# Links from step rows, scaled segments ahead of the copies, and two gather tiles by indirect DMA

## The chip, the cores and the metric

The kernel runs on one core of one Trainium2 chip. The metric is the time of one execution on the device in microseconds; the time before is the median of three runs. In the profile, PE is TensorE's matmul, PEld its weight load, DVE is VectorE, ACT is ScalarE, POOL is GpSimd and SP is SyncE, which here only issues DMAs.

## The reference

There are 256 nodes with 512 features and 4352 edges (`src`, `dst`, sorted by `dst`). Four layers follow each other, each on the layer norm of `x` and added to `x`:

```python
# layer 1: diffusion over the graph
h = x @ W + b
adj = zeros(256, 256); adj[src, dst] = 1; adj[dst, src] = 1; adj += eye
adj = adj / max(adj.sum(1), 1)
out = dw[0] * h; cur = h
for i in range(3):
    cur = adj @ cur; out += dw[i + 1] * cur
x = x + relu(out)
# layer 2: 16 experts of width 64, weighted by a two-level routing
x = x + sum_e tw[:, e] * ((silu(xn @ W1[e]) * (xn @ W3[e])) @ W2[e])
# layer 3: 64 paths over the edges; a segment is 32 of the 512 features
x1 = xn[src]                                  # gather, 4352 rows
for p in range(64):
    edge_out[:, i3[p]] += coef[p] * x1[:, i1[p]] * x2[:, i2[p]]
x = x + zeros(256, 512).at[dst].add(edge_out) # scatter
# layer 4: a mixture with 64 small experts, each picks one of 16 tokens
```

What matters for the change is `adj` in layer 1 (a 1 wherever any edge has that source and destination, however many edges do) and the gather and the products of layer 3.

## The kernel before

All five engines have a program of their own, written out by hand in order, and synchronise by semaphores. An instruction waits at the head of its engine's queue, and what stands behind it waits too.

**Layer 1.** The edges form 34 tiles of 128. For each tile VectorE makes two one-hot matrices in bf16, 128 edges by 256 nodes: `src_oh` (L644) and `dst_ohb` (L646), by comparing the row 0..255 (`iota_b`) with the edge's index. TensorE's `count` (L1008) adds up `src_oh`^T `dst_ohb` over all tiles in two banks, so that each entry counts the edges of a pair. `link_b` (L666) is this count compared with 0.5. TensorE adds its transpose (L1044, L1045), VectorE makes `adj` and its row sums (L683), `cmat` (the rows scaled, L691), and the two series matrices; `square` (L1032) makes the higher powers, and the diffusion is one product `series` x `cur` (L1055), where `cur` is the projection `h` (L1023) plus the bias (L694, L708). `project` is eight pairs of matmul instructions, four for each half of the nodes. TensorE's queue holds, in this order: broadcasts of the source indices (L999), sixteen fillers `keep_warm` (L976, a matmul with zeros), counts of tiles 0 to 8, the transposes of `xn` (L984), counts of tiles 9 to 16, six projections, counts of tiles 17 to 33, symmetric sum, two projections, two squares, diffusion. `src_t` (L674) is the transposed source one-hot for the gather, made from the broadcasts for ten tiles.

Then VectorE and ScalarE form the next layer norm (L716, L626, L451, L634) while TensorE runs 34 fillers, transposes the first half, runs 6 more, and transposes the second half.

**Layer 2.** Eight chunks of 128 hidden features: TensorE makes gate and up (L1073), ScalarE the Silu (L489), VectorE the product (`hidden`, L813) and the routing weight (L828, four in all); the down projection is 32 instructions L1097, sixteen for each half of the nodes, each chunk a pair. Behind the last Silu ScalarE loads the square-root table again (L492) and takes the root for each half of the nodes (L451).

**Gather.** `xn` is written to DRAM (`xn_rows`, L366) and split into three bf16 parts (`xparts`). The tiles of block 0, ten, are gathered by TensorE: six matmuls L1102 for each tile (two halves of the nodes times three parts). Eight tiles have a bank each: first all tiles' first half, then the second half part by part, and tiles 8 and 9 at the end. ScalarE copies the even tiles (L502), VectorE the odd ones (L850) to `x1g[0]`. Ahead of the copies ScalarE converts five destination one-hots to fp32 (L507, `dst_oh`) and VectorE clears `rest_sums[1]` (L845). The tiles of blocks 1 and 2 come from `xn_rows` by GpSimd's indirect DMA (L424, `gather_rows`), one for each tile.

**Path blocks.** Blocks of 10, 14 and 10 tiles. For each of the 64 paths a product goes to one of 12 slots. A path is either direct, where VectorE multiplies both segments and the coefficient in one operation (L874), or ScalarE scales the edge segment into the slot (L526) and VectorE multiplies it with the gathered segment (L879). The first `DIRECT[b]` paths of a block are direct, 16, 16 and 0 before. TensorE adds the product of the first `KEPT[b]` tiles (8, 6, 4) to the bank sums (L1178, L1181), VectorE adds the rest (L889) in SBUF. The scatter matmuls of the block before (L1129) are spread over the paths of the next. Between two blocks ScalarE copies the bank sums out (`copy_sums`, L536, L541). Slots lie in `prod` (5), `xn` (2), `xparts` (3) and `src_t` (2).

**Layer 4** and the store follow; the change leaves them as they are.

## Time and profile before

| | us |
|---|---|
| median of 3 runs | 295.93 (295.72 to 295.97) |
| the profiled execution, its own time | 295.56 |
| its span, first to last instruction | 293.3 |
| diffusion ends / gate and up matmuls start | 36.06 / 43.9 |
| first product of block 0 / of block 1 | 101.08 / 139.66 |
| VectorE busy / ScalarE busy / TensorE busy | 223.4 / 141.3 / 278.1 |

An engine's share is no measure of what it holds up: a stage has to be read where it ends. Fillers count as busy TensorE. The durations below come from the profiled execution; where an engine overlaps two instructions, a row shows the full time of each, and the pitch is read from the starts of neighbours.

### The profile page before, as it was taken

What the parts mean: (1) busy time and instruction counts of PE and PEld (TensorE: products, weight loads), DVE (VectorE), ACT (ScalarE), POOL (GpSimd) and SP (SyncE); (2) the same over time, 40 slices, a digit from 0 to 9 for tenths busy, and PEclk for the clock granted to TensorE, in tenths of its full rate; (3) what the DMA queues carried; (4) which work ended last, traced back from release to release, by engine and by line L of the source; (5) the groups of instructions that cost most, each with busy time, mean ns of one, the idle gap of its engine ahead of it and who ended that gap; (6) DMA issues with size and microseconds to landing.
All of it is one profiled execution on the core that took longest, in us unless ns stands there. A gap on an engine that the chain in (4) does not pass through costs nothing.

```text
span 293.3 us, 5671 instructions
## 1 busy us (share of the span) xinstructions
PE 278.1 (95%) x1711; PEld 193.5 (66%) x1711; DVE 223.4 (76%) x644; ACT 141.3 (48%) x279; POOL 36.7 (13%) x49
## 2 busy tenths in 40 slices
PE   4897799999999899999999999999999999999995
PEld 3754498888444388999678777665666654578632
DVE  5977648243256899999999999999999987955221
ACT  3200132110224358992538786579989819422220
POOL 3000030023003770000870000000000000000000
PEclk9999999999999999999999999999999999999999
DMA  6699960000002774242452000004544429000001
GB/s 206 233 407 420 428 296 0 0 2 1 0 36 70 198 201 140 79 141 76 131 158 72 2 1 1 2 16 136 154 145 144 146 77 349 6 0 2 2 2 72
DMA packets 12287, 33.39 MB, mean 114 GB/s; under 512 B 3297, under 2 KB 3298, under 8 KB 12002
## 3 DMA queue, kind: packets, MB, share of 16 engines
q1 hardware_dynamic: 10338, 26.73, 25.2%
q0 software_dynamic: 1920, 6.29, 7.5%
q8 instruction: 15, 0.25, 0.3%
q14 instruction: 14, 0.11, 0.1%
HBM read 31.97 MB, written 1.05 MB: 113 GB/s over the span
## 4 chain that ended last, share of the span: by engine, by line
PE 82%; DVE 7%; ACT 5%; issue 2%; DVEq 1%; DMA 1%; ACTq 0%; SPq 0%
PE psum L1178 15%; PE psum L1129 12%; PE psum L1073 10%; PE psum L1181 7%; PE psum L1097 5%; PE psum L1102 4%; PE psum L976 4%; PE psum L1008 3%; PE psum L1244 3%; PE psum L1257 2%; PE psum L1263 2%; PE psum L1023 2%; PE psum L1136 2%; DVE big L889 2%; PE psum L1169 1%
## 5 line engine op out<-in xcount | busy, mean ns | idle before, releaser
L1129 PE MATMUL psum<-big,dst_oh 128*128 128x512 f32 x104 | 48.8, 593 | 0.0
L526 ACT ACTIVATE prod<-edges,coef_b 128x320 f32 (+1 forms) x65 | 35.7, 588 | 12.8 <-PE psum L1181 10.7
L879 DVE TENSOR_TENSOR prod<-big,prod 128x320 f32<-128x320 f32 (+1 forms) x65 | 34.8, 535 | 0.5 <-issue 0.3
L424 POOL DMA_INDIRECT big<-xn_rows,big x24 | 26.9, 1119 | 59.3 <-DVE prod L879 29.0
L1178 PE MATMUL psum<-prod,ident 128*128 128x128 f32 x160 | 31.8, 296 | 0.2 <-DVE prod L879 0.2
L1178 PEld LDWEIGHTS psum<-prod,ident 128*128 128x128 f32 x160 | 23.9, 190 | 7.9 <-issue 6.6
L1073 PE MATMUL psum<-edges,big 128*128 128x256 f32 x128 | 28.3, 380 | 0.0
L1129 PEld LDWEIGHTS psum<-big,dst_oh 128*128 128x128 f32 x104 | 18.0, 191 | 13.5 <-issue 13.4
L889 DVE TENSOR_TENSOR big<-big,prod 128x64 f32 (+2 forms) x80 | 26.6, 333 | 0.0
L1073 PEld LDWEIGHTS psum<-edges,big 128*128 128x128 f32 x128 | 24.1, 190 | 3.5 <-DVE edges L813 0.3
L526 ACT ACTIVATE xparts<-edges,coef_b 128x320 f32 (+1 forms) x41 | 22.6, 587 | 2.9 <-PE psum L1181 1.6
L879 DVE TENSOR_TENSOR xparts<-big,xparts 128x320 f32<-128x320 f32 (+1 forms) x41 | 21.9, 534 | 0.5 <-issue 0.3
L1178 PE MATMUL psum<-xparts,ident 128*128 128x128 f32 x96 | 19.5, 298 | 0.8 <-DVE xparts L879 0.7
L1181 PE MATMUL psum<-prod,ident 128*128 128x128 f32 (+1 forms) x110 | 19.9, 262 | 0.0
L526 ACT ACTIVATE xn<-edges,coef_b 128x320 f32 (+1 forms) x26 | 14.8, 589 | 4.0 <-PE psum L1181 3.6
L1181 PEld LDWEIGHTS psum<-prod,ident 128*128 128x128 f32 x110 | 16.7, 192 | 0.0
L1178 PEld LDWEIGHTS psum<-xparts,ident 128*128 128x128 f32 x96 | 14.1, 190 | 3.7 <-issue 3.2
L889 DVE TENSOR_TENSOR big<-big,xparts 128x192 f32 (+2 forms) x48 | 16.3, 339 | 0.0
L976 PE MATMUL psum<-iota_b,zero_b 128*128 128x256 bf16 x118 | 16.2, 293 | 0.0
L526 ACT ACTIVATE src_t<-edges,coef_b 128x320 f32 (+1 forms) x28 | 15.6, 584 | 1.0 <-PE psum L1178 0.6
L879 DVE TENSOR_TENSOR src_t<-big,src_t 128x320 f32<-128x320 f32 (+1 forms) x28 | 14.9, 532 | 0.0
L489 ACT ACTIVATE edges<-psum 128x256 f32<-128x256 f32 x8 | 3.1, 384 | 24.2 <-PE psum L1073 18.6
(199 smaller groups left out, 510.8 us busy)
## 6 DMA issues: line engine op xcount, KB each, us to landing
big<-in_w SPq DMA_DIRECT2D x3, 2048.0 KB, 16.1
edges<-in_f SPq DMA_DIRECT2D x11, 512.0 KB, 3.3
edges<-in_edge SPq DMA_DIRECT2D x1, 3584.0 KB, 23.9
edges<-in_edge SPq DMA_DIRECT2D x1, 2560.0 KB, 23.4
edges<-in_edge SPq DMA_DIRECT2D x5, 512.0 KB, 3.5
edges<-in_f SPq DMA_DIRECT2D x1, 2560.0 KB, 9.9
big<-in_gnn_w SPq DMA_DIRECT2D x1, 1024.0 KB, 6.3
xs<-in_x SPq DMA_DIRECT2D x1, 512.0 KB, 3.9
```

What stands on the lines that cost most here:

```text
L424: nc.gpsimd.indirect_dma_start(out=x1g[b % 2][:, i, :], out_offset=None, in_=xn_rows, in_offset=bass.IndirectOffsetOnAxis(ap=idx_i[:, 0, F ...
L526: nc.scalar.activation(slot(n)[:, 0:BLOCKS[b], :], segment(edges[:, FIRST[b]:FIRST[b] + BLOCKS[b], :], single_column(words, p)), ACT.Copy, ...
L879: nc.vector.tensor_tensor(v, segment(xg[:, 0:tiles, :], first_column(words[b], p)), v, ALU.mult).then_inc(mults, 1)
L889: nc.vector.tensor_tensor(v, v, slot(n)[:, KEPT[b]:BLOCKS[b], :], ALU.add).then_inc(sums, 1)
L976: mm(to[:, 0:N], zero_b[:], iota_b[:], start=True, stop=True)
L1008: last = mm(bank[4 + h][:, 0:N], src_oh[:, t, h * P:(h + 1) * P], dst_ohb[:, t, :], start=t == 0, stop=t == T - 1)
L1073: last = mm(bank[2 + c % 4][:, n * N:(n + 1) * N], w[:, kc, c * P:(c + 1) * P], xnT[:, kc, :], start=kc == 0, stop=kc == KC - 1)
L1097: last = mm(bank[2 + h], hT[:, c, h * P:(h + 1) * P], w2_sb[:, c, :], start=c == 0, stop=c == HC - 1)
L1102: last = mm(gather_bank(t), src_t[:, h, t * P:(t + 1) * P], xparts[:, k, h, :], start=h == 0 and k == 0, stop=h == H - 1 and k == 2)
L1129: last = mm(bank[2 + h], dst_oh[:, n % DR, h * P:(h + 1) * P], tile_sums(b, t), start=False, stop=False)
L1178: last = mm(path_sums(to), ident[:], product[:, 0:PT].rearrange("p t u -> p (t u)"), start=False, stop=False, skip_group_check=True)
L1181: last = mm(more_sums(b, to), ident[:], product[:, PT:KEPT[b]].rearrange("p t u -> p (t u)"), start=False, stop=False, skip_group_check=True)
```

## The change

1. **Steps in place of one-hots for the links.** The destination one-hot is replaced, for the counts, by a row of 258 columns that changes its value behind column `dst` (`steps`). ScalarE makes it by Sign for two tiles in three (+1 and -1), VectorE by a comparison for the third (1 and 0). A column of the sum differs from its right neighbour exactly where an edge ends in it, so `link_b` is now the comparison of the counts with their copy shifted by one (`shifted`, in the place of `cmat`). The destination one-hots, which the scatters need, are made later, behind `hidden(4)` to `hidden(7)`.
2. **TensorE's order in layer 1.** Six fillers at the start in place of sixteen between broadcasts; counts 9 to 17, one projection, counts 18 to 33, two projections, symmetric sum, two, square, two, square, one, diffusion. The fillers in front of the next transposes are 29 and 2 in place of 34 and 6. VectorE's order behind `cmat` follows.
3. **Gather.** TensorE gathers eight tiles; tiles 8 and 9 of block 0 come by two indirect DMAs at the head of GpSimd's queue. The second half's second and third part run tile by tile. Half of `rest_sums[1]` is cleared by GpSimd.
4. **Direct paths** are 0, 8 and 0. ScalarE scales paths 0 to 3 ahead of its gather copies; the first two slots are now free parts of `prod`, the next two lie in `xn`. The five `dst_oh` conversions and ScalarE's path words stand ahead of the third table load.

```diff
-    PE_TILES = BLOCKS[0]
+    PE_TILES = 8
-    DIRECT = [16, 16, 0]
+    DIRECT = [0, 8, 0]
+    FREE_SLOTS = 2
-    OH_A, OH_B = 5, 9
+    OH_A, OH_B = 7, 9
+    STEP_W = N + 2
...
+        def by_vector(t):
+            return t % 3 == 2
...
             def gather_rows(b):
-                if b == 1:
+                if b == 0:
                     pool.wait_ge(xn_out, 16 * H)
-                else:
+                if b == 2:
                     pool.wait_ge(mults, NP * (b - 1))
-                for i in range(BLOCKS[b]):
+                for i in range(0 if b else PE_TILES, BLOCKS[b]):
...
             nc.gpsimd.memset(rest_sums[0], 0.0).then_inc(cleared[0], 1)
+            nc.gpsimd.memset(rest_sums[1][:, 4:, :], 0.0).then_inc(cleared[1], 1)
...
+            gather_rows(0)
             gather_rows(1)
             gather_rows(2)
```

ScalarE:

```diff
             nc.scalar.activation(root[:, H:H + 1], eps[:], ACT.Sqrt)
-            copy_broadcast(0, QT)
+            scalar_tiles = [t for t in range(T) if not by_vector(t)]
+            def make_steps(lo, hi):
+                for t in scalar_tiles[lo:hi]:
+                    nc.scalar.activation(steps[:, t, :], iota_w[:], ACT.Sign, bias=idx_f[:, 2, t:t + 1], scale=-1.0)\
+                        .then_inc(steps_a, 1)
+            act.wait_ge(idx_ready, 3)
+            make_steps(0, 8)
             for h in range(H):
                 root_of_variance(0, h)
+            copy_broadcast(0, 2)
+            make_steps(8, 12)
             copy_xnT(0, xnT)
...
+            make_steps(12, T)
+            copy_broadcast(2, QT)
+            act.wait_ge(cnt_ps, 1)
+            nc.scalar.activation(shifted[:, 0, :], bank[4][:, 1:N + 1], ACT.Copy).then_inc(shift_a, 1)
...
+            act.wait_ge(packed, 3)
+            words = load_words(act, ROW_PATHS, COL_PATHS)
+            act.wait_ge(dst_hot, T)
+            for n in range(DR):
+                nc.scalar.activation(dst_oh[:, n, :], dst_ohb[:, scatter_tile[n], :], ACT.Copy).then_inc(dst_made, 1)
             nc.scalar.activation(root[:, H:H + 1], eps[:], ACT.Sqrt)
...
-            act.wait_ge(onehot, 2 * T)
-            for n in range(DR):
-                one_hot(n)
-            for t in range(0, BLOCKS[0], 2):
+            for n in range(FREE_SLOTS + XN_SLOTS):
+                scale(n)
+            for t in range(0, PE_TILES, 2):
                 copy_gathered(t)
```

VectorE:

```diff
             def one_hots(lo, hi):
                 for t in range(lo, hi):
                     nc.vector.tensor_scalar(src_oh[:, t, :], iota_b, idx_f[:, 0, t:t + 1], None, ALU.is_equal)\
                         .then_inc(onehot, 1)
-                    nc.vector.tensor_scalar(dst_ohb[:, t, :], iota_b[:], idx_f[:, 1, t:t + 1], None, ALU.is_equal)\
-                        .then_inc(onehot, 1)
+                    if by_vector(t):
+                        nc.vector.tensor_scalar(steps[:, t, :], iota_w[:], idx_f[:, 2, t:t + 1], None, ALU.is_le)\
+                            .then_inc(steps_v, 1)
...
-            for h in range(H):
-                dve.wait_ge(cnt_ps, 1)
-                nc.vector.tensor_scalar(link_b[:, h, :], bank[4 + h][:, 0:N], 0.5, None, ALU.is_gt).then_inc(link_ready, 1)
+            dve.wait_ge(cnt_ps, 1)
+            nc.vector.tensor_copy(shifted[:, 1, :], bank[5][:, 1:N + 1]).then_inc(shift_v, 1)
+            for h in range(H):
+                dve.wait_ge((shift_a, shift_v)[h], 1)
+                nc.vector.tensor_tensor(link_b[:, h, :], bank[4 + h][:, 0:N], shifted[:, h, :], ALU.is_gt)\
+                    .then_inc(link_ready, 1)
...
+                if c >= 4:
+                    dst_one_hots((c - 4) * T // (HC - 4), (c - 3) * T // (HC - 4))
...
-            nc.vector.memset(rest_sums[1], 0.0).then_inc(cleared[1], 1)
+            nc.vector.memset(rest_sums[1][:, 0:4, :], 0.0).then_inc(cleared[1], 1)
...
                     if b == 0:
-                        dve.wait_ge(gathered, copied_before(tiles))
-                        dve.wait_ge(xn_out, 16 * H)
+                        dve.wait_ge(gathered, PE_TILES // 2)
+                        dve.wait_ge(row_in[b], 16 * (tiles - PE_TILES))
```

TensorE:

```diff
-                        keep_warm(bank[5], ((34, 6), (18, 2))[stage - 1][h])
+                        keep_warm(bank[5], ((29, 2), (18, 2))[stage - 1][h])
...
+            pe.wait_ge(const, 2)
+            keep_warm(bank[3], 6)
...
-                if q == 2:
-                    keep_warm(bank[3], 16)
...
-            count(OH_B, T // 2)
-            project(0, 0, KC)
-            project(1, 0, KC // 2)
-            count(T // 2, T)
+            count(OH_B, 18)
+            pe.wait_ge(xnT_ready, 2)
+            pe.wait_ge(w_in, 16)
+            project(0, 0, 1)
+            count(18, T)
+            project(0, 1, 3)
             pe.wait_ge(link_ready, H)
...
-            project(1, KC // 2, KC)
+            project(0, 3, KC)
+            project(1, 0, 1)
             square(bank[1], adj, cmat, s2_ps, cmat_ready)
+            project(1, 1, KC - 1)
             square(bank[4], cmat, series2, s3_ps, series2_ready)
-            pe.wait_ge(h_ready, H)
+            project(1, KC - 1, KC)
...
-            for k in range(3):
-                pe.wait_ge((part_a, part_a, part_r)[k], (3, 4, 4)[k])
-                for t in range(8):
-                    gather_part(t, 1, k)
-            for t in range(8, BLOCKS[0]):
-                gather(t)
+            pe.wait_ge(part_a, 3)
+            for t in range(8):
+                gather_part(t, 1, 0)
+            pe.wait_ge(part_a, 4)
+            pe.wait_ge(part_r, 4)
+            for t in range(8):
+                gather_part(t, 1, 1)
+                gather_part(t, 1, 2)
```

## Rows read from the trace of the kernel before

**Rows 1.** The page's part 4, shares of the span by engine.
```profile
PE 82%; DVE 7%; ACT 5%; issue 2%; DVEq 1%; DMA 1%; ACTq 0%; SPq 0%
```

**Rows 2.** Windows by stage: stretch, length, each engine's busy us (instructions), clock, DMA.
```profile
core 0: us, PE busy (x) PEld busy (x) DVE busy (x) ACT busy (x) POOL busy (x), PEclk, DMA share, GB/s
101.00:111.90 10.90, 10.79 (x68) 8.28 (x66) 10.55 (x31) 5.27 (x10) 7.40 (x8) 1.00 0.71 196
111.90:139.60 27.70, 27.25 (x195) 25.16 (x194) 26.93 (x97) 20.93 (x39) 0.06 (x1) 1.00 0.33 104
139.60:154.60 15.00, 15.00 (x92) 10.34 (x91) 14.78 (x32) 7.27 (x14) 12.25 (x10) 1.00 0.51 146
154.60:194.00 39.40, 38.59 (x257) 29.87 (x256) 39.40 (x92) 29.57 (x56) 0.04 (x1) 1.00 0.04 13
```

**Rows 3.** The chain that ended last, piece by piece: start us, us, what.
```profile
4.76 3.41 PE psum L976 x16
...
14.24 5.15 PE psum L1023 x12
...
19.39 3.73 PE psum L1008 x34
...
26.42 1.90 PE psum L1032 x8
...
32.39 3.67 PE psum L1055 x8
...
36.06 3.71 PE psum L976 x34
...
86.99 12.96 PE psum L1102 x60
...
195.33 0.91 ACT xparts L526 x2
```

**Rows 4.** Timeline, first 40 us: start us, us, engine, line, operation.
```profile
0.73 1.28 ACT L467 ACT_TABLE_LOAD   x1 [0.73 <-PEq L1285]
...
3.25 0.26 DVE L650 CAST idx_f<-big 128x68 f32<-128x68 int32 x1 [3.25 <-DMA big<-in_dst]
...
19.73 0.29 DVE L644 TENSOR_SCALAR big<-iota_b,idx_f 128x256 bf16<-128x256 bf16 x1
...
19.93 0.29 DVE L646 TENSOR_SCALAR big<-iota_b,idx_f 128x256 bf16<-128x256 bf16 x1
...
23.21 0.76 DVE L666 TENSOR_SCALAR edges<-psum 128x256 bf16<-128x256 f32 x2 [2.99 <-PE psum L1008]
...
38.54 0.55 DVE L634 TENSOR_SCALAR xn<-xs,mv,rstd 128x512 f32<-128x512 f32 x1
```

**Rows 5.** Groups by form, 101 to 140.5 us: line, operation, count, busy us, mean ns.
```profile
L526 ACT ACTIVATE prod<-edges,coef_b 128x320 f32 x20 | 11.1, 562 | 7.6 <-PE psum L1181 6.6 <-issue 0.3
...
L879 DVE TENSOR_TENSOR prod<-big,prod 128x320 f32<-128x320 f32 x20 | 9.8, 490 | 0.3 <-issue 0.3
...
L874 DVE SCALAR_TENSOR_TENSOR prod<-big,coef_b,edges 128x320 f32 x9 | 4.9, 550 | 0.6 <-DVE big L850 0.4
```

**Rows 6.** Timeline from the down projection to the gather.
```profile
73.10 13.90 PE L1097 MATMUL psum<-big,edges 128*128 128x512 f32 x32
...
73.71 0.42 DVE L813 TENSOR_TENSOR edges<-edges,psum 128x256 f32<-128x256 f32 x1 [3.03 <-ACT edges L489]
...
74.24 0.69 DVE L828 TENSOR_TENSOR edges<-edges,psum 128x512 f32<-128x512 f32 x1
...
81.83 0.29 ACT L451 ACTIVATE root<-mv,eps 128x1 f32<-128x1 f32 x1 [6.64 <-DVE mv L627]
...
91.73 1.62 ACT L507 ACTIVATE dst_oh<-big 128x256 f32<-128x256 bf16 x5
```

**Rows 7.** Timeline of the gather and the first products.
```profile
93.82 0.95 POOL L424 DMA_INDIRECT big<-xn_rows,big  x1 [0.30 <-issue]
...
101.08 1.01 DVE L874 SCALAR_TENSOR_TENSOR prod<-big,coef_b,edges 128x320 f32 x2 [0.41 <-DVE big L850]
```

**Rows 8.** DMA issues by line, with the median us from issue to landing.
```profile
big<-xn_rows,big POOLq DMA_INDIRECT x24, 3.8
```

More of the change, by code:

```diff
@@ L107, in extra_slots @@
             return room[:, 0:n * BMAX * U].rearrange("p (s t u) -> p s t u", s=n, u=U)
-        slots = [prod[:, i] for i in range(OWN_SLOTS)]
-        for room, n in ((xn[:].rearrange("p h d -> p (h d)"), XN_SLOTS),
-                        (xparts[:].rearrange("p k h d -> p (k h d)").bitcast(F32), PART_SLOTS),
+        slots = [prod[:, i] for i in range(OWN_SLOTS - FREE_SLOTS, OWN_SLOTS)]
+        slots += [extra_slots(xn[:].rearrange("p h d -> p (h d)"), XN_SLOTS)[:, i] for i in range(XN_SLOTS)]
+        slots += [prod[:, i] for i in range(OWN_SLOTS - FREE_SLOTS)]
+        for room, n in ((xparts[:].rearrange("p k h d -> p (k h d)").bitcast(F32), PART_SLOTS),
                         (src_t[:].rearrange("p h n -> p (h n)").bitcast(F32), SLOTS - OWN_SLOTS - XN_SLOTS - PART_SLOTS)):
@@ L152, in graph_and_experts @@
         sum_room = [take([BLOCKS[0], D]), late_sums]
-        dst_ohb = take([T, N], BF16)
+        step_room = take([T * STEP_W], BF16)
+        steps = step_room.rearrange("p (t n) -> p t n", n=STEP_W)
+        dst_ohb = step_room[:, 0:T * N].rearrange("p (t n) -> p t n", n=N)
         idx_i = take([2, T], I32)
@@ L713, in _ @@
                     .then_inc(series_ready, 1)
+            dve.wait_ge(h_ps, 2)
+            nc.vector.tensor_tensor(cur[:, 1, :], bank[3], bias_b, ALU.add).then_inc(h_ready, 1)
             for h in range(H):
@@ L1005, in count @@
                 for t in range(lo, hi):
-                    pe.wait_ge(onehot, 2 * (t + 1))
+                    pe.wait_ge(onehot, t + 1)
+                    if by_vector(t):
+                        pe.wait_ge(steps_v, sum(by_vector(i) for i in range(t + 1)))
+                    else:
+                        pe.wait_ge(steps_a, sum(not by_vector(i) for i in range(t + 1)))
                     for h in range(H):
-                        last = mm(bank[4 + h][:, 0:N], src_oh[:, t, h * P:(h + 1) * P], dst_ohb[:, t, :],
+                        last = mm(bank[4 + h][:, 0:STEP_W], src_oh[:, t, h * P:(h + 1) * P], steps[:, t, :],
                                   start=t == 0, stop=t == T - 1)
@@ L1011, in count @@
                     last.then_inc(cnt_ps, 1)
-            for q in range(QT):
-                if q == 2:
-                    keep_warm(bank[3], 16)
+            for q in range(2):
                 broadcast(q)
@@ L1018, in _ @@
             transpose_xn(0)
-            pe.wait_ge(w_in, 16)
+            for q in range(2, QT):
+                broadcast(q)
             def project(h, lo, hi):
@@ L1105, in gather_part @@
                     last.then_inc(gat_ps, 1)
-            def gather(t):
-                if t % 2 == 0:
-                    pe.wait_ge(gathered, copied_before(t - 7))
-                else:
-                    pe.wait_ge(gathered_odd, (t - 7) // 2)
-                for h in range(H):
-                    for k in range(3):
-                        gather_part(t, h, k)
             def scatter(b, n, t):
@@ L1170, in _ @@
                     for _ in range(2 if b else 0):
-                        mm(bank[4][:, 0:N], zero_b[:], iota_b[:], start=False, stop=False, skip_group_check=True)
+                        mm(bank[4][:, 0:N], zero_b[:], iota_b, start=False, stop=False, skip_group_check=True)
                 for p in range(NP):
@@ L1184, in _ @@
                     if KEPT[b] > PT and b and p % 2:
[L1185 removed]
+                        mm(bank[4][:, 0:N], zero_b[:], iota_b, start=False, stop=False, skip_group_check=True)
                     if p in scatter_at:
```

87 lines of the change are left out of this document (46 added, 41 removed).

## The prediction

> **What bounds the kernel now.** I read the chain that ended last first: TensorE holds four fifths of it [rows 1]. A share is an average, so I then read the chain piece by piece over the first 45 us, where most of the edit lies [rows 3], the timeline around its operations [rows 4, 6, 7], and the stages of the path blocks with the busy time of each engine [rows 2]. The reader is to see four places. (a) Up to 23.12 us the counts L1008 wait in TensorE's queue behind twelve projection instructions L1023 (5.15 us), although VectorE had made its last one-hot at 20.2 us [rows 3, 4]. (b) From 23.12 us to the end of the diffusion matmuls at 36.06 us TensorE waits twice for VectorE: 0.9 us for the links and 1.5 us before L1055. (c) Sixty gather matmuls follow the down projection, 12.96 us [rows 3], and the first product starts only at 101.08 us [rows 7]. (d) In block 0 and block 1 VectorE is busy nearly all the time: 10.55 of 10.90, 26.93 of 27.70, 14.78 of 15.00, 39.40 of 39.40 us [rows 2]. TensorE looks as busy there, but its groups only follow the products. The gate and up matmuls, the down projection, block 2 and the last stage are TensorE's own work and the edit leaves them.
>
> **Part 1, links by steps.** VectorE made 68 one-hots before the counts could end, one each 0.20 us [rows 4]. Now it makes 34 source one-hots and 11 step rows, 45 in all, and one small cast more: 23 x 0.197 = 4.5 us less, so it ends at 20.2 - 4.5 + 0.2 = 15.9 us. ScalarE gets 23 Sign activations of 128x258 with a bias column. No row shows Sign. Nearest from below: the 128x256 copies L507, five in 1.62 us, 0.32 us each [rows 6]; from above: the 128x320 scaling L526 with a scale column, 0.56 us alone [rows 5] and 0.455 us each in a pair that runs without waits [rows 3]. Its form is the nearer one; 62 columns fewer leave 0.41 us, which I take: 23 x 0.41 = 9.4 us. ScalarE starts them at 3.9 us (indices at 3.25 us and three small VectorE operations), and between them lie two roots (0.5), two broadcast copies (1.1) and two copies of xnT (1.1), with a wait for the transposes of about 0.3: 3.9 + 9.4 + 3.0 = 16.3 us. The counts are now fed from both engines, and with one projection pair ahead of them instead of twelve instructions they end at about 16.7 us, against 23.12. With 0.32 us a row VectorE decides and it is 16.3; with 0.50 it is 18.4.
>
> Behind the counts I add up TensorE's new order in the durations of [rows 3]: projections 1.72, symmetric sum 0.6, projections 1.72, square 1.90, projections 1.72, square 1.90, last projection 0.86, together 10.4 us, then L1055 3.67 us: 14.1 us to the end of the diffusion against 36.06 - 23.12 = 12.9 before. VectorE must stay under this cover. The link now takes a copy (0.42) and two compares behind it, 1.2 us instead of 0.8 [rows 4]; the projections hide it, and would cost 0.4 us if they didn't. The first half of h is added before the second square ends; the second half is late by about what the first L1055 pair takes. So the diffusion ends at 16.7 + 14.1 = 30.8 us: 5.3 us earlier.
>
> The fillers L976 between diffusion and transposes go from 34 and 6 to 29 and 2. Before, the first transposes followed the fillers at 39.8 us [rows 3], while their input was finished at 39.1 us [rows 4]. Five fillers fewer (0.55 us) are given back nearly whole, and of four fewer in the second group (0.44 us) a part is waited for the second half's input, which follows the first by 0.65 us: together 0.65 us. Part 1 gives 5.9 us, between 4.0 (Sign at 0.50) and 6.3.
>
> **What is moved under the expert stage.** The 34 destination one-hots (34 x 0.197 = 6.7 us) now stand behind hidden(4) to hidden(7), some 1.7 us each. VectorE has room: it idles 3.03 us before the last L813. What is queued behind the last nine is the weighting L828, at 74.24 us now, then at about 76.0, done 76.7. The down projection starts at 73.10 us and needs it for its thirteenth instruction, at 73.10 + 12 x 0.43 = 78.3 us [rows 6]: 1.6 us of cover. ScalarE gets the path words, the wait for the one-hots and five copies (1.62 us) ahead of its table load (1.28): free at about 79.3, needed at 81.83 [rows 4, 6]. I cost all of it at nothing; without the cover it would be at most 1.8 us. GpSimd's longer memset lies in its idle time.
>
> **Part 2, two tiles by GpSimd.** Twelve gather matmuls of 0.216 us go: 2.6 us [rows 3]. The second half's parts are now finished tile by tile, so the copies spread over the matmuls: the last copy follows the last matmul as before (0.69 us), then 0.41 us to the first product. The first product, counted from the same start of the gather, moves from 101.08 to 98.4 us, 2.7 us. It now needs the two rows too. The queue's second indirect DMA was issued at 93.82 us; at 3.8 us to landing the second lands at 97.6 [rows 7, 8], 0.8 us before it is wanted, so nothing; a landing 1 us later would cost 0.2 us. Every DMA of block 1 stands 2.5 us later in GpSimd's queue; that queue is empty from 111.9 to 139.6 us [rows 2], which hides it. SyncE's queue keeps its order; its transfers for block 2 wait for counts of products and so move with them. VectorE's memset ahead of the copies is halved, so it cannot cost.
>
> **Part 3, no direct paths in block 0, eight in block 1.** ScalarE scales four paths before its gather copies (it waited there), the rest behind them. Block 0's first 16 paths took 10.9 us, 0.68 each; the other 48 took 27.7, 0.577 each [rows 2]. 16 x 0.10 = 1.6 us. From below, the bare difference of the operations, 550 against 490 ns [rows 5], would give 1.0 us. ScalarE must scale one path per 0.577 us; a pair takes 0.91 us [rows 3], so it stays ahead, with slots to spare. Block 1: 16 direct paths in 15.0 us, 0.94 each; the next 46 in 39.4, 0.86: 8 x 0.08 = 0.6, of which I take 0.5, as ScalarE copies bank sums at that block's start.
>
> **The page that speaks against.** Rows: the square-root table was loaded once, 1.28 us, and Copy ran behind it without another load [rows 4]. The Trainium skill, "ScalarE: Activation LUTs", section "Table sets: the hidden batching unit", says that cheap functions (it names relu, copy, identity and abs) are in every set and that each set switch costs a load; it doesn't name sign there. By that rule, if Sign had a set of its own, the time would be as in rival 1; no run here shows it yet.
>
> **Sum.** 5.9 + 2.7 + 1.6 + 0.5 = 10.7 us off the profiled span of 293.3: 282.6. That execution took 295.56 us, 2.3 more than its span, so 284.9; the median, 295.93, lies 0.4 higher: 285.2 us.
>
> **Rivals.**
> 1. Sign needs another table than Sqrt. ScalarE's order is Sign, Sqrt, Sign; the first load hides before the indices, two of 1.28 us lie in its sequence, which sets the counts' end: +2.6, 287.8 us. For it: no Sign in the trace. Against it: Copy and Relu needed no load.
> 2. The clock rises late. TensorE ran the first 16 fillers at 0.213 us and later ones at 0.109 [rows 3], which is its 1.2 and its 2.4 GHz level (the granted clock column shows 1.00 throughout). Sixteen fillers at 4.76 us become six at 2.1 us, and TensorE then idles about 1 us for the normalisation. If the counts behind that run at the lower level, the 32 last ones cost 0.1 us more each: +3.4, 288.6 us.
> 3. The other side: the same level holds up to the diffusion's end. Counts, projections, squares and diffusion behind the transposes are about 20 us at the upper level [rows 3]; doubled, less 2 us of waits: +18, 303 us. It turns slower once more than 10.7 of these 20 us run at the lower level. Against it: once the counts come slower than their inputs, TensorE is busy without a gap, which is what raised the clock before.
> 4. The gather's gain is lost: rows or VectorE's word load arrive 2.7 us late, 287.9 us. Point of decision: the second row 3.5 us later than now, or ScalarE unable to keep 0.577 us a path.
>
> **How the numbers follow.** The forecast 285.2 has 0.70 (own range 283.2 to 287.0: part 1 between 4.0 and 6.3, part 3 between 1.0 and 2.5). Rival 1 0.10, rival 2 0.08, rival 4 0.08, rival 3 0.03, an unnamed loss of the whole gain 0.01. A range of 283.0 to 288.5 leaves out less than 2 in 10. This kernel can be told from no change from about 0.2% (0.6 us) on. Only rival 3 lies on the slower side: faster 0.96, no change 0.01, slower 0.03.
>
> **What would show it.** Right: L1008 ends near 16.7 us with the last Sign just before; diffusion ends near 31; L1097 starts near 67; the first product comes 11.4 us behind its end, not 14.1; DVE pitch in block 0 0.577 us from the first path. Wrong: a table load between Signs, L1008 at 0.21 us each behind the transposes, the first product released by a DMA, VectorE in block 0 waiting for ScalarE, or L1097 waiting for L828.

## The result, and the profile after

| | before | after |
|---|---|---|
| median, us | 295.83 (295.63 to 295.97, 4 runs) | 282.95 (282.94 to 282.96, 4 runs) |
| after / before | | 0.9565, 95% interval 0.9549 to 0.9582 |
| profiled execution: own time, span | 295.56, 293.3 | 282.94, 281.1 |
| counts end | 23.12 | 16.38 |
| diffusion ends | 36.06 | 30.19 |
| gate and up matmuls start | 44.05 | 37.32 |
| gather starts | 86.99 | 80.27 |
| first product | 101.08 | 91.58 |
| block 1's first product | 139.66 | 127.99 |
| block 2's first product | 196.54 | 184.35 |

The change is 12.9 us faster. I forecast 10.7 us and 285.2 us; the time lies 0.05 us below my range (283.0 to 288.5) and 2.25 us below the forecast.

The moments are read from the chain of work that ended last; the timeline puts the first gate and up matmul 0.15 us earlier, at 43.89 and 37.17 us, and the experiments below are compared by it.

The lines that answer to those of before follow. First the shares of the chain that ended last [rows 1]: the bound is where it was.

```profile
PE 84%; DVE 7%; ACT 5%; issue 2%; DVEq 1%; DMA 1%; ACTq 0%; SPq 0%
```

The same chain, piece by piece, up to the gather and the first product [rows 3] (start us, us, what):

```profile
9.79 2.17 PE psum L1064 x18
11.96 0.87 PE psum L1078 x2
12.84 3.54 PE psum L1064 x32
16.38 1.72 PE psum L1078 x4
...
26.50 0.86 PE psum L1115 x2
...
27.37 2.81 PE psum L1115 x6
30.19 3.17 PE psum L1026 x29
...
80.27 10.38 PE psum L1162 x48
90.64 0.02 issue
90.67 0.70 DVE big L900
91.37 0.14 issue
```

L1064 are the counts, L1078 the projections, L1115 the diffusion, L1026 the fillers, L1162 the gather. Two things are to be seen. The pieces from 9.79 us to the end of the diffusion follow each other without a hole, where before TensorE waited three times for VectorE: 0.92 us for the links, 0.58 us before the second square and 1.51 us before the diffusion. (The prediction names only the first and the third.) And each pair of the last counts takes 3.54 / 16 = 0.22 us, the same pace as when the counts were never late [rows 3]: TensorE waits for nobody there.

The timeline of that stretch [rows 4] shows the new engine at work (start us, us, engine, line, operation):

```profile
0.74 1.28 ACT L483 ACT_TABLE_LOAD   x1 [0.74 <-PEq L1337]
...
3.74 3.31 ACT L489 ACTIVATE big<-iota_w,idx_f 128x258 bf16<-128x258 bf16 x8 [1.26 <-DVE idx_f L697]
...
6.96 0.58 ACT L467 ACTIVATE root<-mv,eps 128x1 f32<-128x1 f32 x2
...
8.40 1.70 ACT L489 ACTIVATE big<-iota_w,idx_f 128x258 bf16<-128x258 bf16 x4
8.48 1.31 PE L1034 MATMUL psum<-ident,xn 128*128 128x128 f32 x8 [0.18 <-DVE xn L672]
...
10.95 4.51 ACT L489 ACTIVATE big<-iota_w,idx_f 128x258 bf16<-128x258 bf16 x11
...
15.28 0.27 DVE L682 TENSOR_SCALAR big<-iota_w,idx_f 128x256 bf16<-128x256 bf16 x1
...
16.41 0.42 DVE L710 COPY edges<-psum 128x256 f32<-128x256 f32 x1 [0.86 <-PE psum L1064]
```

A Sign takes 4.51 / 11 = 0.41 us, and Sign, Sqrt and Sign follow each other with no table load between them. The load at 0.74 us is ScalarE's only one before 35.01 us. The last Sign ends at 15.46 us and VectorE's last one-hot at 15.55 us, both ahead of the counts' end at 16.38.

Under the expert stage the destination one-hots stand ahead of the weighting (L878, which was L828) [rows 6]:

```profile
57.99 4.24 DVE L691 TENSOR_SCALAR big<-iota_w,idx_f 128x256 bf16<-128x256 bf16 x8
...
66.37 10.04 PE L1157 MATMUL psum<-big,edges 128*128 128x512 f32 x23
...
68.27 1.84 DVE L691 TENSOR_SCALAR big<-iota_w,idx_f 128x256 bf16<-128x256 bf16 x9
70.03 0.67 DVE L878 TENSOR_TENSOR edges<-edges,psum 128x512 f32<-128x512 f32 x1
70.15 1.64 ACT L527 ACTIVATE dst_oh<-big 128x256 f32<-128x256 bf16 x5 [3.19 <-DVE big L691]
```

The path blocks [rows 2]: stretch, length, busy time of each engine, clock, DMA share.

```profile
91.58:100.70 9.12, 9.12 (x70) 8.07 (x70) 9.12 (x33) 9.12 (x21) 6.99 (x8) 1.00 0.69 198
100.70:128.00 27.30, 26.96 (x193) 24.93 (x193) 26.48 (x97) 20.77 (x39) 4.83 (x6) 1.00 0.51 157
```

VectorE (the third column of busy times) works the whole of the first stretch, and ScalarE beside it. The first stretch holds the products of seventeen paths, not sixteen, so a pitch (the time from one path's product to the next one's) has to be read from the start of the seventeenth product. Here it is after the change, and then before it:

```profile
100.27 0.49 DVE L929 TENSOR_TENSOR prod<-big,prod 128x320 f32<-128x320 f32 x1
```
```profile
111.92 0.48 DVE L879 TENSOR_TENSOR prod<-big,prod 128x320 f32<-128x320 f32 x1
```

With the milestones of the table: the first sixteen paths take 8.69 us, 0.543 each, where they took 10.84, 0.678 each. The next forty-eight, which the edit doesn't touch, take 27.72 us and took 27.74, 0.578 each. So all of block 0's gain lies in its first sixteen paths.

### The profile page after: what moved, and what is told of

The parts are those of the page before. It is cut to its first block, busy times and chain, and to the rows that moved or that the text cites. A ratio compares the mean times of both kernels' runs of the same rounds, so it can differ in the third digit from the quotient of the medians.

```text
span 281.1 us, 5714 instructions
## 1 busy us (share of the span) xinstructions
PE 271.3 (96%) x1678; PEld 188.9 (67%) x1678; DVE 223.6 (80%) x654; ACT 160.7 (57%) x325; POOL 45.2 (16%) x52
## 4 chain that ended last, share of the span: by engine, by line
PE 84%; DVE 7%; ACT 5%; issue 2%; DVEq 1%; DMA 1%; ACTq 0%; SPq 0%
PE psum L1230 16%; PE psum L1179 13%; PE psum L1133 10%; PE psum L1233 8%; PE psum L1157 5%; PE psum L1162 4%; PE psum L1026 3%; PE psum L1296 3%; PE psum L1309 3%; PE psum L1315 3%; PE psum L1078 2%; PE psum L1186 2%; PE psum L1064 2%; DVE big L939 2%; PE psum L1221 2%
## 5 line engine op out<-in xcount | busy, mean ns | idle before, releaser
L564 ACT ACTIVATE prod<-edges,coef_b 128x320 f32 (+1 forms) x77 | 43.2, 594 | 10.3 <-PE psum L1233 8.8
L437 POOL DMA_INDIRECT big<-xn_rows,big x26 | 33.5, 1288 | 52.0 <-DMA xn_rows<-xn 23.5
L929 DVE TENSOR_TENSOR prod<-big,prod 128x320 f32<-128x320 f32 (+1 forms) x77 | 40.5, 527 | 0.7 <-ACT prod L564 0.3
L564 ACT ACTIVATE xparts<-edges,coef_b 128x320 f32 (+1 forms) x45 | 24.4, 586 | 1.5 <-PE psum L1230 0.9
L929 DVE TENSOR_TENSOR xparts<-big,xparts 128x320 f32<-128x320 f32 (+1 forms) x45 | 23.5, 522 | 0.3 <-issue 0.3
L1233 PE MATMUL psum<-prod,ident 128*128 128x64 f32 (+1 forms) x110 | 19.8, 262 | 0.0
L564 ACT ACTIVATE xn<-edges,coef_b 128x320 f32 (+1 forms) x32 | 17.8, 591 | 0.2 <-PE psum L1230 0.2
L929 DVE TENSOR_TENSOR xn<-big,xn 128x320 f32<-128x320 f32 (+1 forms) x32 | 16.8, 525 | 0.1
L564 ACT ACTIVATE src_t<-edges,coef_b 128x320 f32 (+1 forms) x30 | 16.4, 581 | 0.6 <-PE psum L1230 0.6
L1233 PEld LDWEIGHTS psum<-prod,ident 128*128 128x128 f32 x110 | 16.7, 192 | 0.0
L929 DVE TENSOR_TENSOR src_t<-big,src_t 128x320 f32<-128x320 f32 (+1 forms) x30 | 15.6, 521 | 0.2 <-ACT prod L564 0.2
```

The source lines that it names most:

```text
L437: nc.gpsimd.indirect_dma_start(out=x1g[b % 2][:, i, :], out_offset=None, in_=xn_rows, in_offset=bass.IndirectOffsetOnAxis(ap=idx_i[:, 0, F ...
L564: nc.scalar.activation(slot(n)[:, 0:BLOCKS[b], :], segment(edges[:, FIRST[b]:FIRST[b] + BLOCKS[b], :], single_column(words, p)), ACT.Copy, ...
L929: nc.vector.tensor_tensor(v, segment(xg[:, 0:tiles, :], first_column(words[b], p)), v, ALU.mult).then_inc(mults, 1)
L1233: last = mm(more_sums(b, to), ident[:], product[:, PT:KEPT[b]].rearrange("p t u -> p (t u)"), start=False, stop=False, skip_group_check=True)
```

## The experiments

There were sixteen runs, in four groups of four, each group on a chip of its own with the kernel before beside it. Before took 300.05, 300.07, 299.04 and 295.25 us in the four groups, not 295.83 in all: why, is the subject of the third group. So a time below stands beside the others of its group, and a part is read from the moments of its own trace (the table's rows above) where something else disturbs the time.

### Group 1: the parts of the first stage, and direct paths

**e1, all steps on VectorE.**
```diff
         def by_vector(t):
-            return t % 3 == 2
+            return True
```


> All 34 step rows on VectorE instead of 23 on ScalarE; everything else as in the changed kernel. Theory A (the gain of the first stage needs the work taken from VectorE): VectorE's 23 rows more, 0.197 us each, end its part at 15.6 + 4.5 = 20.1 us, the counts end at about 20.4 instead of 16.4, and the time is 282.95 + 4.0 = 287.0 us. Theory B (the gain is TensorE's new order alone, the counts being fed in time anyway): the counts end within 0.5 us of now, and the time stays under 283.5 us.

297.19 us (before 300.05). The counts end at about 20.6 us, and gate and up start at 41.40 and not 37.17 (timeline): ScalarE's 23 Signs are worth 4.2 us.

**e2, the old order on TensorE** (twelve projections ahead of the counts' second half, then both squares).
```diff
-            count(OH_B, 18)
+            count(OH_B, T // 2)
...
-            project(0, 0, 1)
-            count(18, T)
-            project(0, 1, 3)
+            project(0, 0, KC)
+            project(1, 0, KC // 2)
+            count(T // 2, T)
```


> TensorE's queue in the first stage as before the change (six projections ahead of the second half of the counts, the last two behind the symmetric sum), the step rows as in the changed kernel. Theory A (both halves of the edit are needed; in the changed kernel TensorE never waits behind the transposes, so only moved waits count): the counts end 4.3 us later (five projection pairs), the links' wait and the wait for the row-scaled matrix come back, and of the 5.9 us at the diffusion's end 3 to 4 are lost: 286 to 287 us. Theory B (the order is worth nothing, the freed VectorE is all): under 283.5 us.

296.37 us. TensorE's timeline shows the waits of before at their old places, and gate and up start at 40.31 us, 3.1 us late:

```profile
16.62 3.93 PE L1064 MATMUL psum<-big 128*128 128x258 bf16 x34
21.81 0.23 PE L1101 MATMUL psum<-edges 128*128 128x128 bf16 x1 [1.26 <-DVE edges L713]
...
26.98 1.99 PE L1087 MATMUL psum<-xparts,edges 128*128 128x256 f32 x8 [0.89 <-DVE xparts L751]
```

Taking away the steps loses 4.2 us and taking away the order 3.1; together the two gave 5.87 us at the end of the diffusion. So each without the other gives only 2.8 and 1.7 us: either edit alone leaves some of the other's wait.

**e3, the old numbers of fillers** (34 and 6 for 29 and 2).
```diff
-((29, 2), (18, 2))
+((34, 6), (18, 2))
```


> 34 and 6 fillers ahead of the second transposes again instead of 29 and 2. Theory A: in the changed kernel the transposes wait 0.2 us for the normalised half, so of nine fillers (0.97 us) 0.8 to 0.9 come back: 283.8 us. Rival (the fillers lie in a wait): 282.95 us.

294.16 us. Gate and up start at 38.03 against 37.17 us: the nine fillers are worth 0.86 us, not the 0.65 of my sum.

**e4, sixteen direct paths in block 0** (the ninth to the twenty-fourth).
```diff
-            return p < DIRECT[b]
+            return p < DIRECT[b] or (b == 0 and 8 <= p < 24)
```


> Paths 8 to 23 of block 0 are direct again (sixteen, as before the change, but eight paths later, so that ScalarE's start is as in the changed kernel). Theory A: VectorE sets the pitch of block 0, 0.68 against 0.567 us a path: + 1.8 us, 284.75 us. Rival (part of block 0's 2.2 us came from the paths prepared ahead of the copies, not from the form): + 1.0 us by the durations alone, 283.95 us.

293.17 us, and e3 less its 0.86 us of fillers comes to the same, 293.3, with all of block 0 scaled. The trace told why the part couldn't be read here: for some 10 us from about 98 us on (102 in e1 and e2) TensorE, VectorE and ScalarE stood nearly still in all four traces of the group. e15 repeats the edit without that.

### Group 2: the gather

**e5, the second half by parts and not tile by tile**: the loops over `t` and `k` in (1, 2) change places. 

> The second half of the gather runs part by part again (all eight tiles for the second part, then all for the third) instead of tile by tile; eight tiles as in the changed kernel. Theory A (the order spreads the copies over the matmuls): the copies start 1.7 us before the end of the matmuls instead of 3.2 and four of 0.6 us stand in each engine, so the first product comes 0.5 us later: 283.45 us. Rival (the copies keep up either way, or the rows of the indirect DMAs set the first product): 282.95 us.

293.36 us (before 300.07). The first product starts at 92.08 us against 91.58: three of VectorE's four copies stand in the chain, behind the forty-first of the 48 gather matmuls.

```profile
80.33 9.03 PE psum L1162 x41
89.36 0.02 issue
89.38 1.90 DVE big L900 x3
91.28 0.73 issue
```

The copies pile up, as the order by parts finishes the tiles together; tile by tile only one is left. The order is worth 0.5 us.

**e6, ten tiles by TensorE.**
```diff
-    PE_TILES = 8
+    PE_TILES = 10
```
with the matmuls of tiles 8 and 9 behind those of the eight. 

> TensorE gathers all ten tiles of block 0 again, tiles 8 and 9 behind the others; the indirect DMAs of block 0 are gone. Theory A: twelve matmuls of 0.216 us more and a copy behind them: the first product 2.6 us later, 285.55 us. Two broadcasts and their share of the transposed one-hot more in the first stage lie beside other work. Rival (the rows of the indirect DMAs arrive just when wanted, so that the gather was worth less): 284 us.

291.98 us, the fastest of its group, though the first product starts at 94.16 us, 2.6 us late. GpSimd issues 14 indirect DMAs in a row here and not 16, and the stretch in which the other engines stand cost 4 us less: 6.1 us against e16, which is this kernel without it, where it costs the changed kernel 10.0 (group 3).

**e7, six tiles by TensorE, four by GpSimd** (`PE_TILES = 6`, the loops over eight tiles cut to it). 

> TensorE gathers six tiles, GpSimd four by indirect DMA. Theory A (the rows are the next limit): the fourth indirect DMA is issued at 89.6 us, lands 3.8 us later at 93.4, and the first product waits for it until about 93.6 instead of 91.58: 285 us, slower than the changed kernel though TensorE has 2.6 us less to do. Rival (rows come in time or the product is not held): 280.4 to 282 us.

295.00 us. Here the rows are late, and the trace names it:

```profile
89.60 0.94 POOL L437 DMA_INDIRECT big<-xn_rows,big  x1 [0.30 <-issue]
```
```profile
93.59 0.89 DVE L929 TENSOR_TENSOR prod<-big,prod 128x320 f32<-128x320 f32 x2 [3.89 <-DMA big<-xn_rows,big]
```

The fourth row is issued at 89.60 us and the product starts 4.0 us later, 2.0 us after that of the change. With two tiles the second DMA is issued at 87.10 us; with the same 4.0 us it lands at 91.1, 0.5 us before the product. My sum had 0.8 us of cover. A third DMA, issued at 88.35 us, would land at about 92.3 by the same price, later than the change's first product; that is an estimate, as no run has three tiles.

**e8, nine one-hots made twice, ahead of the last weighting.**
```diff
+                if c == 7:
+                    for t in range(25, T):
+                        nc.vector.tensor_scalar(dst_ohb[:, t, :], iota_b, idx_f[:, 1, t:t + 1], None, ALU.is_equal)...
```


> The last nine destination one-hots, behind the last product of the expert stage, are made twice, which puts 1.9 us of VectorE's work ahead of the last routing weight. Theory A (cover of 1.0 us: in the changed kernel the weight is done at 70.70 us and the thirteenth instruction of the down projection needs it at 71.7): + 0.9 us, 283.85 us. Theory B (cover of 1.6 us, as predicted): + 0.3 us, 283.25 us. Theory C (the weight is not waited for at all): 282.95 us.

294.67 us. The added one-hots take 1.84 us, the down projection waits 0.96 us for the weighting, and the first product moves by 1.23 us, to 92.81: the moved one-hots hide with 0.6 to 0.9 us to spare, not the 1.6 of the prediction.

```profile
72.66 5.85 PE L1162 MATMUL psum<-big,edges 128*128 128x512 f32 x13 [0.96 <-DVE edges L883]
```

### Group 3: the stretch that disturbed the runs

**e9, the changed kernel unedited; e10, the kernel before unedited**, on one chip; e10 is a single execution, for its trace. 

> The changed kernel, unedited, on the chip of the other runs, on which the kernel before took 300.05 us and not 295.83. In all runs so far TensorE, ScalarE and VectorE crawl together from about 97 us to the end of GpSimd's row of indirect DMAs (109.4 us with 2+14 of them, 105.7 with 14): single instructions with 1 to 6 us between them and nothing that released them. If that belongs to this chip and not to my edits, the changed kernel shows it here too: 293.2 us (the run with more fillers, 294.16, less the 0.86 us that they measured), stages up to 97 us as in its first profile. If the edits caused it, 283 to 284 us and no crawl.

> The kernel before, unedited, for its trace on this chip. If the crawl comes from the row of indirect DMAs, it is seen here too, but shorter, as the row (14, from 92.1 us) ends at about 112 us and the first product starts only at 101.1: some 4 us lost between 103 and 112 us, 300 us in all, and everything up to 101 us as in [rows 3, 6, 7]. If it comes from something else, the 4 us are spread over the span.

**e11, block 1's indirect DMAs issued one for every four products.**
```diff
                 for i in range(0 if b else PE_TILES, BLOCKS[b]):
+                    if b == 1 and i:
+                        pool.wait_ge(mults, 4 * i)
                     nc.gpsimd.indirect_dma_start(
```


> One edit: block 1's indirect DMAs are issued one for every four products of block 0 and not back to back, the last at about 121 us, before block 1's first product at 128. Theory: the crawl comes from that dense row; then it is gone or nearly so and the time is 283.0 to 285 us on this chip. Rival: the crawl has another cause (a place in the code, the chip's clock); then it stays where it is, 293 us. Second rival: it lasts as long as any of the DMAs run, now until 121 us, and the time is over 300 us.

The changed kernel took 292.97 us here, 10 us more than in its first runs, and the kernel before 299.04 (299.10 in e10). Spread over block 0, the DMAs brought it to 282.92 us (0.9455 of before, interval 0.9439 to 0.9471). The windows of e9 and then of e11 show the stretch and its end:

```profile
92.00:97.50 5.50, 5.50 (x43) 4.64 (x43) 5.50 (x20) 3.43 (x8) 4.28 (x5) 1.00 0.70 192
97.50:109.30 11.80, 3.39 (x13) 2.52 (x13) 2.87 (x10) 1.42 (x3) 7.11 (x8) 0.64 0.68 198
109.30:115.00 5.70, 5.70 (x32) 5.70 (x31) 4.94 (x18) 5.70 (x14) 0.00 (x0) 0.56 0.24 61
```
```profile
97.50:109.30 11.80, 11.61 (x85) 10.69 (x84) 11.53 (x42) 11.29 (x23) 5.49 (x5) 1.00 0.59 167
```

In 11.8 us TensorE issued 13 matmuls in e9 and 85 in e11; VectorE and ScalarE fell with it, and only GpSimd went on, with eight DMAs at its usual pace and the DMA engines 68% busy. The waits of e9 in that stretch name no releaser inside the core (engine and line, what it waited for, us in total, times, longest):

```profile
ACT xn L564 <- remote: 5.8, 1, 5.8
DVE xn L929 <- ACT xn L564: 5.8, 1, 5.8
PEld psum L1233 <- issue: 4.7, 4, 1.8
...
PE psum L1233 <- issue: 4.4, 4, 1.7
```

"issue" is time in which an engine waits for nothing that the profile shows. The last DMA of e9's row is issued at 105.79 us, and the engines run again from 109.3:

```profile
105.79 0.95 POOL L437 DMA_INDIRECT big<-xn_rows,big  x1 [0.30 <-issue]
```

TensorE's clock falls with it: 0.64 of 2.4 GHz granted over the slow stretch, in which it was busy 3.4 of 11.8 us, and 0.56 in the 5.7 us behind it, close to the level of 1.2 GHz. The kernel before shows the same in e10, from about 106 to 112 us, shorter as its row is: up to its first product (100.82 us) it is as in [rows 7], and block 0 takes 42.4 us for 38.6. So the stretch is a matter of the dense row, in three of the groups; it isn't the edit's. The change only makes it cost more, as its row has two DMAs more and lies beside products for 17 us (92.0 to 109.3) and not 11.5 (100.8 to 112.3): 10 us of its time, and some 4 of before's.

What starves the engines isn't shown. The first runs of the changed kernel issued the same row at the same pace and lost nothing. A supply of instructions that the row holds up would fit waits without a releaser, but no run tests it; nor does one tell the chip from the hour or from where the data lay, since each group had its own.

**e12, the spread and two edits more**: no direct paths in block 1 (with the copies of block 0's banks ahead of its ninth path), and the normalisation behind two one-hots fewer.
```diff
-    DIRECT = [0, 8, 0]
+    DIRECT = [0, 0, 0]
-    OH_A, OH_B = 7, 9
+    OH_A, OH_B = 5, 7
```


> The spread of e11, and two edits more whose places don't touch: no direct paths in block 1, and the normalisation behind five and seven one-hots, not seven and nine. Block 1 against e11: eight direct paths of 0.94 us each become 0.86: 0.5 us earlier, if ScalarE keeps 0.86 us a path; if its bank copies get in the way, nothing. Counts: their end moves from 16.38 by 0.2 us at most by my reading that TensorE is busy without a gap behind the transposes and VectorE's last one-hot (15.55 us) holds it next; if the normalisation alone set it, by 0.6 us. Together 0.5 to 1.1 us less than e11.

285.90 us, 3 us slower than e11 where 0.5 to 1.1 us faster was expected. The earlier normalisation ends the counts 0.35 us later, at 16.73: the transposes start only 0.23 us earlier (8.25 for 8.48), and four count matmuls that ran ahead of them now run behind. In block 1 ScalarE stands still with block 2's row of DMAs running, and VectorE waits for it:

```profile
136.57 0.67 ACT L566 ACTIVATE prod<-edges,coef_b 128x448 f32 x1 [0.68 <-remote]
143.08 0.67 ACT L566 ACTIVATE prod<-edges,coef_b 128x448 f32 x1 [5.84 <-remote]
```
```profile
143.95 0.62 DVE L931 TENSOR_TENSOR prod<-big,prod 128x448 f32<-128x448 f32 x1 [3.63 <-ACT prod L566]
```

Either the row, or ScalarE's lack of room, could be behind it. The last group decides on the second.

### Group 4: the parts undisturbed

Before, with its dense row, took 295.25 us on this chip, so the stretch seems to be absent here anyway. In the four runs block 1's row is spread, and none of their traces shows it.

**e13, both rows spread** (block 2's DMAs too, one for every four products). 

> Block 1's and block 2's indirect DMAs both one for every four products. Against the spread of block 1 alone (282.92 us): in block 2's dense row one DMA on GpSimd took 6.39 us where the others took 0.94 to 1.56; if that too is the crawl, falling on GpSimd itself, it is gone, and as VectorE didn't wait for it the time stays within 0.4 us of 282.9. If block 1's direct paths and ScalarE's bank copies have nothing to do with the row, the same time as well; this run is the base for the next one.

**e14, the same without direct paths in block 1**, the copies of block 0's banks ahead of the ninth path.
```diff
-    DIRECT = [0, 8, 0]
+    DIRECT = [0, 0, 0]
...
-                if b == 1 and p == 0:
+                if b == 1 and p == 8:
                     copy_sums(0, 0, 8)
```


> Both rows spread, and no direct paths in block 1 (its first eight are scaled by ScalarE; the copies of block 0's banks stand before the ninth). In the run before, with block 2's row dense, ScalarE stood still for 5.84 us behind 137.2 us, VectorE waited 3.63 us for it, and the kernel lost 3 us. Theory: that standstill is the crawl again, falling on ScalarE; with the row spread it is gone and eight paths at 0.86 and not 0.94 us give 282.3 to 282.9. Rival: ScalarE has no room there for eight more scalings beside eight bank copies (4.1 us); then the wait stays and the time is 284.5 to 286.

282.94 and 282.15 us. The edit that went with 3 us more in e12 gains 0.8 us here (0.9558 of before against 0.9586), and ScalarE's standstill is gone: it was not lack of room. That the dense row of block 2 made it is likely but not shown, as e14 ran on another chip than e12. e14 is the fastest kernel of the study.

One part of e13's expectation fell: with block 2's row spread GpSimd's long DMA doesn't go. Its traces have 6.64 us at 135.26 us and a longer one yet, at no cost in time:

```profile
145.89 22.66 POOL L439 DMA_INDIRECT big<-xn_rows,big  x1 [1.19 <-DVE src_t L931]
```

**e15, the spread of block 1 and sixteen direct paths in block 0.** 

> The spread of block 1's row, and sixteen of block 0's paths direct again (the ninth to the twenty-fourth), as the first sixteen were before. My sum has 1.6 us for sixteen paths (0.10 us each): 284.5. The bare difference of the operations gives 1.0: 283.9. The whole shift that block 0 showed, 2.17 us: 285.1. If only the start of the block costs (the first paths while ScalarE fills its slots), less than 1.0.

284.97 us, 2.03 more than e13 (which differs only in block 2's row). The timeline of VectorE shows a direct path at 0.69 us and a scaled one at 0.54 to 0.60:

```profile
104.64 0.55 DVE L926 SCALAR_TENSOR_TENSOR xparts<-big,coef_b,edges 128x320 f32 x1
...
105.33 0.55 DVE L926 SCALAR_TENSOR_TENSOR xparts<-big,coef_b,edges 128x320 f32 x1
...
107.34 0.48 DVE L931 TENSOR_TENSOR prod<-big,prod 128x320 f32<-128x320 f32 x1
...
107.94 0.49 DVE L931 TENSOR_TENSOR prod<-big,prod 128x320 f32<-128x320 f32 x1
```

The sixteen direct paths run from 96.10 to 107.34 us, 0.70 each; scaled, in e13, the same paths run from 95.87 to 105.06 us, 0.575 each. That makes 2.05 us, 0.13 a path, and the first direct one starts 0.23 us late: block 0 is 2.3 us longer (38.65 for 36.37). Of the values expected, the shift that block 0 had shown (2.17 us, 285.1) is the nearest.

**e16, the spread of block 1 and ten tiles by TensorE** (as in e6). 

> The spread of block 1's row, and all ten tiles gathered by TensorE again, parts and copies as in the change otherwise. My sum: twelve matmuls of 0.216 us come back, 2.6 us: 285.5, with two copies more on two engines at most 0.4 on top. If the order by parts of the second half was worth part of the 2.7 us, less comes back, 284.9 or under.

285.90 us. The chain has 60 gather matmuls in 12.96 us, one copy behind them, and the first product at 94.17 and not 91.59 us: 2.6 us, and 3.0 in the time against e13. The last 0.4 us arises behind block 2's first product, which is 2.57 us late (186.92 for 184.35) where the span is 3.0 longer; its cause is open.

## Why the prediction missed

| term of the sum | forecast, us | measured, us | by |
|---|---|---|---|
| counts end | 6.4 | 6.74 | milestones; e1 |
| counts to the end of the diffusion (a loss) | -1.1 | -0.87 | milestones; e2 |
| fillers | 0.65 | 0.86 | e3 |
| gather and copies | 2.7 | 2.78 | e5, e7, e16 |
| block 0 without direct paths | 1.6 | 2.17 | e15 |
| block 1, eight direct paths fewer | 0.5 | 0.52 | milestones |
| one-hots under the expert stage | 0 | 0 | e8 |
| outside the span | 0 | 0.42 | own time less span: 2.26, then 1.84 |
| median above the profiled time (counted against the gain) | -0.4 | 0 | 295.93 against 295.56 before |

The gain came from the parts that were forecast, no rival came about, and one reason (what sets the counts' end) was wrong; several sizes fell short, all on one side, which is why small misses left the range. Measured less forecast, the rows add up to the 2.25 us by which the time lies below the forecast, within rounding.

- **"16 x 0.10 = 1.6 us"** is the largest, and the step that failed most. The price of a direct path, 0.68 us, held. That of a scaled one was taken as the mean of the forty-eight later paths of before, 0.577 us [rows 2], but the sixteen paths that change form run at 0.543: 2.15 us. The forty-eight ran at 0.578 before and after. In e15, where the ninth to the twenty-fourth path change form, a direct path costs 0.13 us more than a scaled one, and not 0.10. What raises the later mean can be seen, if not why: three steps of 0.88 to 0.91 us, and from the twenty-third to the forty-sixth path a pitch that mostly alternates between 0.545 and about 0.595 us. ScalarE doesn't make this, as each of their segments was scaled over 4 us before its product; what does is not shown. Block 1's forecast, from the same kind of row, held.
- **"3.9 + 9.4 + 3.0 = 16.3 us"**, ScalarE's end, was taken to set the counts' end (16.7), and that reason was wrong. The Signs took 9.3 us, but what lies between them 2.4 and not 3.0, and ScalarE started at 3.74. TensorE runs from 9.79 to 16.38 without a hole, and both makers are done 0.8 us earlier. e12 bears it out: giving TensorE its transposes sooner, at the price of counts run before them, ended the counts later. e1 shows the other half, 4.2 us lost when VectorE makes all steps and is the bound again.
- **"14.1 us to the end of the diffusion"** took 13.81: the symmetric sum was 0.45 us and not 0.6, the second square 1.73 and not 1.90. The diffusion's own matmuls took 3.69, as priced. The links' second operation hid, as forecast.
- **"Five fillers fewer (0.55 us) are given back nearly whole"**: e3 against the change has the first transposes at 33.74 and 33.27 us and the second at 34.84 and 33.98, so the five gave 0.47 us, as said, and the four 0.39, of which I had counted 0.1. The second half's input was ready (33.87 us in the timeline) before its transposes' turn.
- **Two small ones outside the argument.** The time around the span fell by 0.42 us. It goes with the change and not with the execution: the own time less the span is 2.23 to 2.35 us in every execution of the kernel before on record, and 1.75 to 1.91 in every one of a kernel with the change. I had no reason to expect it and know none. And I added the 0.37 us by which the median lay above before's profiled execution; the changed kernel's four times lie within 0.02 us, and nothing of the sort was there.

What was moved under the expert stage cost nothing, as forecast, but with half the cover: the one-hots pushed the weighting to 70.03 us, done at 70.70, against about 71.5 where the down projection's thirteenth instruction wants it (66.37 + 12 x 0.43).

**The rivals.** Sign in a table of its own (rival 1) isn't so: 23 Signs around two roots, without a load. The rule of the Trainium skill, "ScalarE: Activation LUTs", section "Table sets: the hidden batching unit", was weighed there because it names relu, copy, identity and abs as being in every set and not sign; here Sign behaves as those do beside Sqrt. The clock (rivals 2 and 3) stayed at 1.00, and the last 32 counts took 0.11 us each, the price of the upper level in [rows 3]. It fell only in and behind the starved stretch of groups 1 to 3. Rival 4's mechanism, rows that land late, was near, 0.5 us away for two tiles; e7 shows it at work with four.

**What the range missed.** Its lower end left 2.2 us for all terms together, below the forecast, but the bounds that the prediction names don't reach so far: part 1 at 6.3 and not 5.9 us and part 3 at 2.5 and not 2.1 make 284.4 us. Both bounds were passed (6.73 and 2.69), and the term outside the span had no bound at all.

## What to carry to other kernels

Before a price is taken from an average pitch, look at the same operations pair by pair in the timeline: 0.54 and 0.69 us were there to be read, and the mean over forty-eight paths hid the first. When work is shared between two makers, ask whether the engine that takes it has become gapless: then neither maker's price matters. And a row of back-to-back indirect DMAs that isn't urgent is better issued at the pace at which its predecessor is consumed: it cost nothing (282.92 and 282.94 us spread, 282.95 for the dense row where nothing disturbed it) and was worth 10 us where the engines starved.

## What was not expected of the hardware

- The same program differs by 10 us between groups of runs, each on its own chip, nearly all of it in the starved stretch (block 0 takes 46.0 us in e9 and 36.4 in the first runs): 282.95 and 292.97 us for the changed kernel, 295.25 to 300.07 for the one before. Inside it TensorE's matmuls start one at a time, mostly 1.4 or 2.1 us apart.
- An indirect DMA's time on GpSimd, 0.94 to 1.56 us elsewhere, became 6.39 us beside block 1's scaled products in the change, 6.64 and 22.66 in e13, and 11.34 in e14, where these products start earlier:

```profile
133.70 1.56 POOL L437 DMA_INDIRECT big<-xn_rows,big  x1 [0.31 <-issue]
135.57 6.39 POOL L437 DMA_INDIRECT big<-xn_rows,big  x1 [0.30 <-issue]
```
```profile
131.03 11.34 POOL L439 DMA_INDIRECT big<-xn_rows,big  x1 [1.86 <-DVE xparts L931]
```

  The rows weren't wanted for another 40 us, so it cost nothing. The Trainium skill, "GPSIMD Engine Reference", section "Key points", says that GpSimd shares its SBUF interfaces with VectorE and names contention with VectorE's instructions in a 2-port mode or with two SBUF inputs. These runs agree as far as the long issues begin beside such products; but other issues beside the same 128x448 products took 0.95 to 1.10 us (from 142.26 us in the change), and block 0's shorter products (128x320) never did it. What makes one issue long is not shown.
- VectorE was slower too beside GpSimd: beside GpSimd's two affine selects (3.64 us from 58.26), eight one-hots took 4.24 us (57.99 us, above), and eight without them, from 66.37 us, 1.64. Only this one pair was seen, and no run takes the selects away.
